# Decode-style attention with a projected residual: weight loads moved earlier, row sums inverted one query head at a time

## The reference

```python
x = x + einsum('bsi,boi->bso', x, weight[adapter_ids])      # 8 x 128 x 512, one 512x512 matrix per batch row
q = einsum('bsd,ed->bse', x, Wq)   # 32 heads of 128;  k, v: 8 heads of 128
q, k = rope(rmsnorm(q) * q_norm_w), rope(rmsnorm(k) * k_norm_w)
kc, vc = k_cache[block_table], v_cache[block_table]          # 16 pages of 32 keys = 512 cached keys
k_all, v_all = concat([kc, k]), concat([vc, v])              # 640 keys; cached ones beyond cache_seqlens masked
probs = softmax(q @ k_all.T / sqrt(128));  o = probs @ v_all
x = x + einsum('bse,de->bsd', o, Wo)
```

## Time and profile before

| | us |
|---|---|
| median of three runs | 1088.78 |
| lowest and highest run | 1084.17, 1089.38 |
| profiled execution, its time | 1084.17 |
| profiled execution, its span | 1082.0 |
| PE busy | 1020.7 (94%) |
| DVE, ACT, POOL busy | 862.3 (80%), 804.8 (74%), 755.2 (70%) |
| mean busy share of the DMA engines in the transposing stage | 0.80 |

### The profile page before, as it was taken

One profiled execution on the slowest core, in us unless ns is written; L12 is line 12 of the kernel. 1 busy time (PEld: TensorE's weight loads), 2 busy tenths in 40 slices (PEclk: granted clock), 3 DMA queues, 4 the chain that ended last, 5 costly groups with the idle time before them and its releaser, 6 DMA issues.

```text
span 1082.0 us, 19618 instructions
## 1 busy us (share of the span) xinstructions
PE 1020.7 (94%) x5500; PEld 866.2 (80%) x5500; DVE 862.3 (80%) x1791; ACT 804.8 (74%) x2094; POOL 755.2 (70%) x794
## 2 busy tenths in 40 slices
PE   6799987999989999999999999999999999999996
PEld 4587776889878888888888888888878888878874
DVE  6565645667779988898888998989888998998883
ACT  4363544666688888888888888988888888988883
POOL 1776655565467877877877877776867877777653
PEclk9899998999999999999999999999999999999999
DMA  6687768988587787888878887778788887787874
GB/s 206 186 250 238 226 189 217 230 238 234 111 153 149 149 164 143 150 164 153 153 150 151 151 157 156 141 163 146 155 150 151 151 157 153 147 158 141 145 155 105
DMA packets 477837, 180.85 MB, mean 167 GB/s; under 512 B 420753, under 2 KB 457762, under 8 KB 475682
## 3 DMA queue, kind: packets, MB, share of 16 engines
q1 hardware_dynamic: 474464, 167.61, 74.2%
q10 hardware_dynamic: 2242, 9.89, 2.9%
q0 software_dynamic: 1024, 2.10, 0.8%
HBM read 109.25 MB, written 35.66 MB: 134 GB/s over the span
## 4 chain that ended last, share of the span: by engine, by line
PE 50%; SPq 21%; DMA 7%; ACT 6%; DVE 6%; issue 6%; POOL 4%; POOLq 0%; ACTq 0%; DVEq 0%
PE S L1217 11%; SPq L391 6%; SPq L401 5%; PE O L1151 5%; SPq L346 4%; PE O L1152 4%; PE O L1153 4%; DMA turned<-pr 3%; PE Q L1151 3%; POOL ptl L512 3%; PE Q L1153 3%; PE Q L1152 3%; PE T L1157 3%; DMA first<-pr 3%; DVE pr L938 3%
## 5 line engine op out<-in xcount | busy, mean ns | idle before, releaser
L918 DVE CUSTOM_DVE_ANT_0 pr<-S,mask,rst 128x640 f32<-128x640 f32 x256 | 225.5, 881 | 47.9 <-PE S L1217 46.3
L938 DVE SCALAR_TENSOR_TENSOR pr<-pr,rc,raw 128x640 f16<-128x640 f32 x208 | 229.7, 1105 | 9.0 <-ACT raw L719 5.2
L734 ACT ACTIVATE pr<-pr,nb 128x640 f32<-128x640 f32 x256 | 211.2, 825 | 26.7 <-DVE nb L918 26.5
L537 POOL TENSOR_TENSOR m<-m 128x512 f32<-128x512 f32 x64 | 111.4, 1741 | 80.8 <-DVE m L966 79.0
L719 ACT ACTIVATE raw<-pr,rc 128x640 f16<-128x640 f32 x208 | 165.8, 822 | 2.3 <-DVE rc L934 2.2
L1151 PE MATMUL O<-pth,vh 128*128 128x512 f32 x256 | 108.4, 423 | 26.0 <-POOL ptl L512 22.2
L679 ACT ACTIVATE Q<-Q 128x128 f32<-128x128 f32 x256 | 68.4, 267 | 81.8 <-DVE m L966 81.8
L512 POOL TENSOR_SCALAR ptl<-first 128x512 fp32r<-128x512 f16 x130 | 96.3, 741 | 44.6 <-DMA first<-pr 35.9
L491 POOL TENSOR_TENSOR kl<-raw,kh 128x512 fp32r<-128x512 f32 x64 | 93.0, 1453 | 47.7 <-ACT kh L619 47.2
L1217 PE MATMUL S<-kh,qh 128*128 128x320 f32 x512 | 122.3, 320 | 3.5 <-DVE nb L918 2.6
L512 POOL TENSOR_SCALAR ptl<-turned 128x512 fp32r<-128x512 f16 x130 | 93.6, 720 | 45.1 <-DMA turned<-pr 36.4
(11 more groups left out here) (114 smaller groups left out, 2695.9 us busy)
## 6 DMA issues: line engine op xcount, KB each, us to landing
raw<-cache_rows SPq DMA_DIRECT2D x112, 256.0 KB, 4.0
cache_rows<-in_kv SPq DMA_DIRECT2D x96, 256.0 KB, 5.1
wraw<-in_wall SPq DMA_DIRECT2D x73, 256.0 KB, 3.3
mask<-mask_rows SPq DMA_DIRECT2D x64, 128.0 KB, 3.5
cache_rows<-in_kv ACTq DMA_DIRECT2D x32, 256.0 KB, 5.4
first<-in_lw SPq DMA_DIRECT2D x28, 256.0 KB, 4.4
acc<-in_x SPq DMA_DIRECT2D x8, 256.0 KB, 4.7
raw<-in_kv SPq DMA_DIRECT2D x128, 16.0 KB, 2.8
```

The source lines that it names most:

```text
L537: e.tensor_tensor(m1[:, :, :], m1[:, :, :], m2[:, :, :], ALU.add).then_inc(g_qadd, 1)
L734: e.activation(pr[:, slot(u, g), :], pr[:, slot(u, g), :], ACT.Exp, bias=nb[:, u % 2, g:g + 1], scale=-1.0, accum_out=sm[:, u % 2, g:g + 1 ...
L918: e.tensor_tensor_reduce(pr[:, slot(u, g), :].rearrange("p (a n) -> p a n", a=2), S[:, :, 0:320], mask[:, u % 2, :].rearrange("p (a n) -> ...
L938: e.scalar_tensor_tensor(out=lower16(u, g), in0=pr[:, slot(u, g), :], scalar=rc[:, u % 2, g:g + 1], in1=upper16[:, g, :], op0=ALU.mult, op ...
```

## The change

Four things are changed. (1) The tables: most chunks are loaded and split one period or so earlier (`LOAD_AT`, `HI_ACT`, `LO_DVE`, `LO_POOL`), with the first chunks of key head 1 left as they were. (2) SP issues the weight loads of a period ahead of the page copies and of the transposes of query heads 0 and 1, not behind them. (3) DVE scales and inverts the row sums one query head at a time, not two. (4) `upper_plane` of query head 2 moves from the start of the next period to the end of its own, behind `exp(i, 3)`; in unit 12 likewise.

```diff
-          0: (-5, 0), 1: (-4, 0), 2: (-4, 1), 3: (-2, 0), 4: (-2, 1), 5: (-2, 0),
-          6: (0, 0), 7: (0, 1), 8: (1, 0), 9: (1, 1)}
+          (1, 0): (-5, 0), (1, 1): (-4, 0), (1, 2): (-4, 1),
+          0: (-6, 0), 1: (-5, 0), 2: (-4, 0), 3: (-2, 0), 4: (-2, 1), 5: (-2, 0),
+          6: (-1, 0), 7: (0, 0), 8: (0, 1), 9: (1, 1)}
...
+           0: (-6, 1), 1: (-5, 1), 2: (-4, 1), 3: (-2, 1), 4: (-1, 0), 6: (-1, 1),
...
-LOAD_AT = {0: -6, 1: -6, 2: -5, 3: -4, 4: -3, 5: -3, 6: -1, 7: -1, 8: 0, 9: 0}
+LOAD_AT = {(1, 0): -6, (1, 1): -6, (1, 2): -5, (1, 3): -4, (1, 4): -3, (1, 5): -3,
+           0: -7, 1: -6, 2: -5, 3: -5, 4: -4, 5: -3, 6: -2, 7: -1, 8: -1, 9: 0}
@@ SP, periods 0 to 11
+                next_weights(i)
                 if NL <= i + 2 < NA:
                     load_v(i + 2)
                 for b, t in copies_of(i):
                     copy_pages(b, t)
-                next_weights(i)
@@ ACT
-                e.wait_ge(v_rc, 2 * (NA + n) + g // 2 + 1)
+                e.wait_ge(v_rc, 2 * NA + G * n + g + 1)
...
                 if turn:
-                    upper_plane(w, 2)
                     upper_plane(w, 3)
...
                     exp(i, 3)
+                    upper_plane(i, 2)
@@ DVE
-            def scaled_recip(u, half):
-                gs = slice(2 * half, 2 * half + 2)
-                e.wait_ge(a_exp, 4 * u + gs.stop)
-                e.tensor_scalar(sm[:, u % 2, gs], sm[:, u % 2, gs], 1.0 / PS, None,
+            def scaled_recip(u, g):
+                e.wait_ge(a_exp, 4 * u + g + 1)
+                e.tensor_scalar(sm[:, u % 2, g:g + 1], sm[:, u % 2, g:g + 1], 1.0 / PS, None,
                                 ALU.mult).then_inc(v_sm, 1)
...
                     largest(i, 1)
+                    scaled_recip(i, 0)
                 output_lo(o)
...
-                    scaled_recip(i, 0)
+                    scaled_recip(i, 1)
                     largest(i, 2)
...
                     largest(i, 3)
+                    scaled_recip(i, 2)
...
                 add_output(o)
                 if real:
-                    scaled_recip(i, 1)
+                    scaled_recip(i, 3)
```

More of the change, by code:

```diff
@@ L63 @@
 HI_ACT = {(0, 6): (1, 0), (0, 7): (1, 1), (0, 8): (1, 1), (0, 9): (2, 0),
-          0: (-5, 0), 1: (-4, 0), 2: (-4, 1), 3: (-2, 0), 4: (-2, 1), 5: (-2, 0),
-          6: (0, 0), 7: (0, 1), 8: (1, 0), 9: (1, 1)}
[L66 to L69, removed]
-LOAD_AT = {0: -6, 1: -6, 2: -5, 3: -4, 4: -3, 5: -3, 6: -1, 7: -1, 8: 0, 9: 0}
[3 rows of a table added]
+LO_DVE = {(0, 6): (1, 1), (0, 7): (1, 1), (0, 9): (2, 1), (1, 4): (-1, 0),
+          5: (-2, 1), 7: (0, 1)}
+LO_POOL = {(0, 8): (1, 1), (1, 0): (-5, 1), (1, 1): (-4, 1), (1, 2): (-3, 0),
+           0: (-6, 1), 1: (-5, 1), 2: (-4, 1), 3: (-2, 1), 4: (-1, 0), 6: (-1, 1),
+           8: (1, 0), 9: (2, 0)}
+LOAD_AT = {(1, 0): -6, (1, 1): -6, (1, 2): -5, (1, 3): -4, (1, 4): -3, (1, 5): -3,
+           0: -7, 1: -6, 2: -5, 3: -5, 4: -4, 5: -3, 6: -2, 7: -1, 8: -1, 9: 0}
 BESIDE = (3, 4, 5, 9)
@@ L808, in _ @@
                     copy_page(*place)
-            for g in range(2):
+            for g in range(3):
                 upper_plane(NA, g)
@@ L925, in recip @@
                 e.reciprocal(rc[:, u % 2, gs], sm[:, u % 2, gs]).then_inc(v_rc, 1)
-            def scaled_recip(u, half):
-                gs = slice(2 * half, 2 * half + 2)
-                e.wait_ge(a_exp, 4 * u + gs.stop)
-                e.tensor_scalar(sm[:, u % 2, gs], sm[:, u % 2, gs], 1.0 / PS, None,
+            def scaled_recip(u, g):
+                e.wait_ge(a_exp, 4 * u + g + 1)
+                e.tensor_scalar(sm[:, u % 2, g:g + 1], sm[:, u % 2, g:g + 1], 1.0 / PS, None,
                                 ALU.mult).then_inc(v_sm, 1)
-                e.wait_ge(v_sm, 2 * (u - NA) + half + 1)
-                e.reciprocal(rc[:, u % 2, gs], sm[:, u % 2, gs]).then_inc(v_rc, 1)
+                e.wait_ge(v_sm, G * (u - NA) + g + 1)
+                e.reciprocal(rc[:, u % 2, g:g + 1], sm[:, u % 2, g:g + 1]).then_inc(v_rc, 1)
             def lower_plane(u, g):
@@ L1086, in _ @@
                 elif i == NA:
-                    scaled_recip(i, 0)
+                    for g in range(3):
+                        scaled_recip(i, g)
                 if 1 < lb < NB:
```

## The result

| | before | changed kernel |
|---|---|---|
| median of 4 runs, us | 1089.08 (1084.17 to 1089.78) | 1101.24 (1098.93 to 1104.15) |
| ratio, 95% interval | | 1.0121 (1.0085 to 1.0158) |
| the profiled execution, us | 1084.2, span 1082.0 | 1106.2, span 1104.4 |
| start of period 13 | 290.7 | 294.2 |
| periods 13 to 62 | 757.9 | 775.4 |

The account below looks back on a forecast made before the run. SP's issuing and PE's 14.5 us floor were taken as close bounds from 290 us on. Terms -7.3, -8 and +2 took 1084.2 to 1070.9, put at 1073 us as a median; 8 in 10 range 1055 to 1090.

Parts of the forecast that it names:

- What bounds the kernel: From 290 us on: PE's floor is 14.5 us a period, SP's issuing 14.1 plus about half per weight load.
- The rival that transfers and not their issue set the pace: From 290 us on, DMA transfers are the limit and reordering SP's loads gains nothing: 1081 us median, chance 0.14.
- Part 2, the gain of 23: Periods from 12: weight loads ahead of the transposes cut SP's cycle to 14.1 to 14.2 us: -23 us.
- What is put between costs nothing up to some 1.4 us: On SP, between keys' load and first transpose: one or two weight loads, 0.53 us each, would fit free.
- the 33: Second stage: the most that could be won, 50 periods x (15.16 - 14.5) us.
- Part 2, the wait of 14: Periods 8h+6: SP waits 3.9 us for chunk 6, making PE 2.4 us late next period, six times: +14 us.
- the slower rival: Periods 8h+6: SP's wait for chunk 6 is paid in full, nothing won elsewhere: 1093 to 1102 us, chance 0.12.
- Part 1, -7.3: Periods 0 to 11: weight loads ahead of the page copies remove most of ACT's 8.87 us wait: -7.3 us.
- What is late next?: First stage: the mask of period 11, with 7.3 us of slack, cuts the gain from 8.3 to 7.3 us.
- Part 3, +2: DVE, each period: two more scalings and inversions add 0.78 us, mostly covered by idle time: +2 us in all.
- Part 4, 0: Upper plane of query head 2 earlier: no gain in itself, 0 us, from -3 to +3.
- What was to show it: Signs in the new trace, among them period 6 about 17.5 us and PE's stalls gathered in periods 8h+7.

Follow-up runs that it names:

- e6: Kernel before, from period 12 on with the mask's load issued behind the keys' load instead of ahead of it; 1068.52 us, ratio 0.981.
- e4: Kernel before, from period 12 on with the keys' load issued by ACT behind exp(i, 1) instead of by SP; 1079.37 us, ratio 0.997.
- e1: Changed kernel with the load of chunk 6 of each key head put at the end of SP's period; 1082.38 us, ratio 0.999 to the kernel before.
- e8: Changed kernel with chunk 6 loaded at the end of SP's period and the mask behind the keys; 1059.81 us, ratio 0.972 to the kernel before.
- e5: Kernel before with only chunk 6 of key heads 2 to 7 loaded a period earlier, right behind the keys; 1100.26 us, ratio 1.011.
- e2: Kernel before with only the single inversions and the earlier upper plane of query head 2; 1083.73 us, ratio 1.000.
- e3: Kernel before with only the new tables and SP's new order of loads; 1098.45 us, ratio 1.015.
- c1: Kernel before with new tables, chunk 6 late, second-stage loads between last transposes and mask, keys issued by ACT behind p_hi(w, 1); 1063.20 us, ratio 0.979.
- c3: c1 with the single inversions and the earlier upper plane as well; 1062.69 us, ratio 0.976 to the kernel before.
- e7: Changed kernel with only the mask's load put behind the keys' from period 12 on; 1072.69 us, ratio 0.985 to the kernel before.

## Why the prediction was wrong, step by step

**What bounds the kernel: right.** SP's issuing set the pace of the second stage, and POOL's `ptl` handed it to PE. Seven tenths of a microsecond off SP's cycle (e6) gave 18.8 us in the stage and 1.9% in the time. The rival that transfers and not their issue set the pace would have had no gain from the swap, and falls as a whole; e4 shows that it holds for what comes next. The Trainium skill ("DMA: Bandwidth & Descriptors", "Issuing engines are not separate DMA queues") says that the time to initiate a DMA is usually small relative to the DMA itself. Here a transpose took 1.28 us to issue, out of 2.7 from issue to landing. e6 speaks against what the prediction drew from the page, since swapping two issues in one queue moved 1.9%, and e4 for it, since a second issuer moved only 0.3%, and its interval reaches 1.000.

**Part 2, the gain of 23: the first step that failed.** "What is put between costs nothing up to some 1.4 us" rested on the earlier trace rows, where SP *waited* 0.9 us for a semaphore between keys and transpose. Waiting was hidden there (and in eight other periods of that trace with a gap of 0.16 to 0.41 us, where the end comes 3.2 to 3.7 us after the keys' start). Issuing another load is not: 0.6 us each, as the table under e6 has it. SP's cycle did not fall from 15.2 to 14.1; the loads were paid in another place. Measured: nothing in the time (e1, ratio 0.999, 0.995 to 1.003). The size had a second flaw: PE was idle only 758 less 736.07 = 21.9 us of the stage, less than the 23 that were to be won; the 33 came from one period of 14.5 us taken as the floor of all. (PE's busy time can shrink as well, since it did in e8, so 21.9 is no strict bound.)

**Part 2, the wait of 14: right in mechanism, and in size by the medians.** The hole was put at 3.9 us and measured 27.7/6 = 4.6. Its price was put at 2.4 a time, 14 in all. By the medians it is 14 us in the changed kernel and 13 in e5 (1100.26 less 1086.83). The profiled executions have more, 20.8/6 = 3.5 and 14.7/6 = 2.5 a time. PE's waits for `ptl` in the six periods of the changed kernel are 15.0/6 = 2.5, near what was forecast; what the prediction left out is the lower clock behind such a wait, which it did count in its part 1.

With no gain beside it, the wait stood alone. This is the slower rival, by its own condition ("if the loads are not covered behind the keys, so that SP's cycle stays at 15.2"), which was given 1093 to 1102 and a chance of 0.12. The measured 1101.24 lies in it, and so does the difference of the medians, 12.2, in its +9 to +18. That is luck in part: of the rival's other terms the -7.3 came to about half in the traces and the +2 to nothing that shows. What spoke for the rival was one row too: SP had no hole at all. What spoke against was the misread wait.

**Part 1, -7.3: the wait went, most of the gain did not come.** ACT's wait is gone, but period 6 took 22.3 us and not 17.5, and period 7 22.0 and not 16.7. The start of period 13 differs from execution to execution: with the old first stage 290.7, 293.7, 293.2, 294.0 and 297.7 (before, e2, e4, e5, e6), mean 293.9; with the new one 294.2, 290.0, 287.2, 284.8, 293.1, 287.3 and 291.8 (changed, e1, e3, c1, c3, e7, e8), mean 289.8. The 4.1 us between the means are barely clear of that spread (95% interval 0.3 to 7.9). Periods 6 and 7 together, which the part was about, take 43.8 us on average in the old and 42.1 in the new, 1.7 less. The time of e1, level with before, shows no gain from it. The failed step is "What is late next?": it looked at the mask of period 11 and found 7.3 us of slack. Period 7's was nearer. In the kernel before that mask was issued at 175.46 and landed 5.4 us later, 9.3 us before its period began at 190.12; with ACT's wait gone the period could begin as soon as the mask is there. In six of the seven traces of the new first stage it landed less than 0.1 us before period 7 began (of the seventh, e3, the landing is not recorded), after 9 to 11 us on its way, and period 7 then took 20.2 to 22.7 us, not 16.7. In the five traces of the old order, where the two weight loads stand between the copies and this mask, it was 5.4 to 7.4 us on its way. Chunk 6's issue of 6.19 us is not its cause: in e8, where that load comes later, `load_v` takes 7.8 us at the same place. Putting the mask ahead of the copies was not tried.

**Part 3, +2: the direction can't be told, the size was smaller.** The operations on one column take 149 and 164 ns, not 222 and 166: 4 x 0.313 less 2 x 0.388 is 0.48 us a period, not 0.78. DVE was busy 674.8/50 = 13.5 us a period, not 14.2. Nothing of it reached the time (e2, c3 against c1), though both runs have part 4 as well.

**Part 4, 0: not contradicted** (e2, together with part 3). Where the order of the loads is good (c3), the two together did no harm and no measured good.

**What was to show it.** The mean period is 15.5 and not under 15.1, and the first transpose ends 4.0 and not 3.4 us after the keys (median): both were named as signs that the prediction or part 2 is wrong. DVE's idle time in the stage, which was to halve, rose from 88 to 101 us. Three signs came as named: the hole on SP in the six periods 8h+6, no wait for any other weight load, and POOL ending PE's waits. Half of those waits, 15.0 of 30.7 us, gathered in the periods 8h+7.

## What to carry to other kernels

In a queue that is itself the bound, moving an issue wins only if its new place is cheaper: measure what an issue costs beside each neighbour, and do not take a stretch that hid a wait as one that hides work. A load moved earlier brings its semaphore wait with it, and everything queued behind stands too; put the one load whose buffer comes free late behind the work that others wait for. After a stall is taken out, look at the very next period first. Price a stall of PE with the lower clock that can follow it, and compare two kernels by the medians of their runs before their single traces.

## What the runs showed of the chip

- The issue behind the keys' load (128-byte pieces) is lengthened by an amount that depends on what it is: a transpose by 1.5 us, a 256 KB weight load by 1.6, the 128 KB mask by 0.6. Two neighbouring instructions swapped took 1.9% off the kernel. Why the mask gets off more lightly no run shows.
- A weight load that follows on a wait, in place of following the keys' issue directly, took 0.33 us (period 30, above).
- Behind a wait of PE of 2.0 to 3.4 us the granted clock was at the lower level, 1.2 GHz, for a while, in four of six cases in the changed kernel; each cost some 1.7 us beside the wait. The length of the wait does not decide it alone: one of 2.0 us brought it there, and one of 2.2 us in e7 did not.
- With the keys issued from a second engine, the transposes issued 2.0 us earlier and landed 0.8 us earlier.
